# Causal attention of a fused two-layer network: the mask moved from TensorE to VectorE, and score rows cut in their middle

## The chip, the cores and the metric

One core of a Trainium2 chip runs the whole network as one program. The metric is the device time of one execution in microseconds (us). The engines of the core work side by side and meet at semaphores: TensorE (PE in the profile, with its weight loads as PEld), VectorE (DVE), ScalarE (ACT), GpSimd (POOL) and SyncE (SP, which here only issues transfers). TensorE writes to PSUM, eight banks of 512 fp32 columns, from which VectorE and ScalarE read.

## The reference, cut to what matters

The network has two layers with an attention-like half and a mixture-of-experts half each, over 2 batches of 1024 tokens with 256 features. The change lies in the causal attention of the second layer: 16 query heads, 4 key/value heads of 128 features, so four query heads share a key head.

```
scores = jnp.einsum('bqhd,bkhd->bhqk', q, k) / np.sqrt(HD)
causal = jnp.tril(jnp.ones((s, s), dtype=bool))
scores = jnp.where(causal[None, None], scores, jnp.finfo(scores.dtype).min)
probs = jax.nn.softmax(scores, axis=-1)
out = jnp.einsum('bhqk,bkhd->bqhd', probs, v).reshape(b, s, H * HD)
return out @ wo
```

## The kernel before, in words

The program is a sequence of stages (a modulation, a Mamba block, a mixture of experts, attention 1, attention 2, another mixture of experts). Each stage is a block of five engine programs, and the next stage starts when all of them are done. The change is in `attn2`, and in two small casts at the end of `attn1`.

`attn2` works through eight groups u = 0 to 7 (2 batches x 4 key/value heads). In a group each of the four query heads has eight row tiles i = 7 to 0 of 128 queries. Because of the causal mask, row tile i needs only the first (i + 1) x 128 keys, so a score is 128 to 1024 columns wide. One order of work, the list `todo` that `schedule()` writes (tokens project, score, turn, value, out, and a few more), is followed by all engines:

- *score* (line 2362, TensorE): q times k for one head and row tile. Each operand is held as a high and a low part in a rounded fp32 format, and three products (high x high, low x high, high x low) are summed in PSUM. The columns are cut at 512, the size of a bank: 640 columns become 512 + 128, 768 become 512 + 256, 896 become 512 + 384. Then a bf16 matmul of the identity with a 128x128 mask tile (0, and -3e38 above the diagonal) adds the mask to the last 128 columns (line 2365).
- VectorE takes the row maximum of the score from PSUM (line 2145) and scales it by -SCALE (line 2146). ScalarE computes the exponential from PSUM to SBUF with this as bias, and its row sum (line 2247). VectorE takes the reciprocal of the sum (2135, 2137). For three of the heads GpSimd multiplies the row by it (2219), for the fourth VectorE does (2138).
- *turn* (2376): four fp32 transposes of 128x128 probabilities, copied to SBUF by ScalarE (2263). *value* (2386): the product with v, an fp32 matmul that runs as two instructions. *out* (2395): the product with wo, added up by VectorE (2192).
- *project* (2339): the q and k projections of the next group, followed by the rotary embedding on VectorE (2176 to 2178), GpSimd (2203, 2208) and ScalarE (2253).

Scores, projections and their like live in PSUM banks 0 to 3, one or two banks each in turn. A score may start only when the exponential that reads the earlier user of its banks is done (`unit_free`). The transposes of row tile i start when all four heads' probabilities are scaled. VectorE carries further chores between scores, most of them in u = 0: the residual and the normalisation of the other batch.

The mask arrives in fp32 as `mask_f`, loaded during attention 1. Two casts on VectorE at the end of attention 1 (lines 1801 and 1802) make the bf16 mask and the bf16 identity.

Of the kernel before, what the change touches and what calls it, by code (L numbers as in the profile page):

```python
# [7 lines left out]
P = 128  # L8
F32 = mybir.dt.float32
BF16 = mybir.dt.bfloat16  # L10
# [3 lines left out]
ALU = mybir.AluOpType  # L14
ACT = mybir.ActivationFunctionType
AX_X = mybir.AxisListType.X

B, L, D = 2, 1024, 256
# [51 lines left out]
def flat(ap):  # L70
    return ap.rearrange("p a b -> p (a b)")
# [1357 lines left out]
class Ahead:  # L1429
# [3 lines left out]
    def __init__(self, ctx, nc, g, hs):  # L1433
        sb = lambda n, s, d=F32: ctx.enter_context(nc.sbuf_tensor(f"h_{n}", s, d))
        self.hs = hs
        self.hT, self.wh = ([sb(n + half, shape, F32R) for half in ("hi", "lo")] for n, shape in (("hT", [P, KC, L]), ("wh", [P, KC, WC])))
        self.wm, self.qk = ([sb(n + half, [P, c, L], F32R) for half in ("hi", "lo")] for n, c in (("wm", REP - 1), ("qk", KC)))
        self.kT = [q[:, 0, :] for q in self.qk]
        self.qT = [[q[:, 1, :], *(w[:, h, :] for h in range(REP - 1))] for q, w in zip(self.qk, self.wm)]
        self.mask, self.ident_b = sb("mask", [P, P], BF16), sb("ident_b", [P, P], BF16)  # L1440
        sizes = (("w_s", KC * WC), ("cos", L), ("sin", L), ("nwb", D), ("mask_f", P))
        at, part = 0, {}
        for n, size in sizes:
            part[n] = g.raw[:, at:at + size]
            at += size
        self.w_s = part["w_s"].rearrange("p (k n) -> p k n", k=KC)
        self.cos, self.sin, self.nwb, self.mask_f = part["cos"], part["sin"], part["nwb"], part["mask_f"]
        self.spare = g.raw[:, at:at + D]
# [9 lines left out]
def attn1(nc, g, pre, fc_w, fc_b, norm_w, wq, wk, wv):  # L1458
# [7 lines left out]
    with ctx:  # L1466
# [25 lines left out]
        s_nb, s_e, s_eh, s_el, s_vs, s_av, s_acc = sem("nb"), sem("e"), sem("eh"), sem("el"), sem("vs"), sem("av"), sem("acc")  # L1492
        s_rot, s_turned, s_rh, s_roped = sem("rot"), sem("turned"), sem("rh"), sem("roped")
        s_plain = [sem(f"plain{k}") for k in range(KC)]
        s_next, s_nh, s_nl, s_bf = sem("next"), sem("nh"), sem("nl"), sem("bf")
        block = ctx.enter_context(nc.Block())

        def hT_of(b):
# [256 lines left out]
        def _(dve):  # L1755
# [38 lines left out]
            def scaled(q):  # L1794
                if q == 0:
                    own.wait()
                    dve.wait_ge(s_next, 16 * 7)
                norm.scaled(hs[:, TB + 4 * q:TB + 4 * q + 4, :], 4 * q, 4, pre.nwb).then_inc(s_xn, 1)

            def small():  # L1800
                dve.tensor_copy(pre.mask[:, :], pre.mask_f)
                dve.tensor_copy(pre.ident_b[:, :], ident[:, :]).then_inc(s_bf, 1)

            chores = {0: [lambda: stats1(0), lambda: stats1(1), lambda: norm.spread(1, False), lambda: fold(0), lambda: norm.inverse(1, 2),
                          lambda: None, lambda: None, lambda: fold(1),
                          *[lambda q=q: norm.centred(hs, x, TB + 2 * q, 2) for q in range(4)],
# [5 lines left out]
                          *[lambda q=q: norm.modulated(hs, 4 * q, 4, CB, ALU.mult) for q in range(2)],  # L1812
                          *[lambda q=q: norm.modulated(hs, 4 * q, 4, SB, ALU.add) for q in range(2)],
                          lambda: norm.stats(hs, 0, TB), lambda: norm.spread(0, True), lambda: None, lambda: None, lambda: None,
                          lambda: norm.inverse(0, 4), lambda: scaled(0), lambda: (scaled(1), small())]}

            def value_rows(b, h, m):
                r = row[b, h, m]
# [90 lines left out]
def attn2(nc, g, pre, wq, wk, wv, wo):  # L1909
# [8 lines left out]
    with ctx:  # L1918
# [1 line left out]
        sem = lambda n: ctx.enter_context(nc.semaphore(f"a2_{n}"))  # L1920
        x, mod, ps, ident = g.x, g.mod, g.ps, g.ident
        SCALE = 1.0 / float(np.sqrt(HD))
        nrm, hs, nwb, w_s, cos, sin, mask, ident_b = g.nrm, pre.hs, pre.nwb, pre.w_s, pre.cos, pre.sin, pre.mask, pre.ident_b
        wo_s = sb("wo", [P, 2, REP, D])
        HI, LO = 0, 1
        ER = 4
# [4 lines left out]
        e = sb("e", [P, 2, REP, L])  # L1931
        side = sb("side", [P, REP, 5 * P])
        ao = sb("ao", [P, 2, REP, P])
        product = pre.cos.rearrange("p (a d) -> p a d", a=4)
        summed = flat(side[:, :, :])[:, 0:TB * D].rearrange("p (a b) -> p a b", a=TB)
        mx, nb, sm, rc = (sb(n, [P, TB * REP]) for n in ("mx", "nb", "sm", "rc"))
        d_x = nc.dram_tensor("a2_dx", [B * L, D], F32, kind="Internal").ap()
        names = ("own", "acc", "res", "xn", "tr", "hT", "hlow", "whigh", "wlow", "unit", "w", "rot", "sum", "high", "rope", "rope_k",
                 "v", "nb", "e", "rc", "en", "en_last", "xout", "xin", "spare", "wo_in",
                 "tp", "eT", "o", "ao", "wo", "hs")  # L1940
        s = {n: sem(n) for n in names}
        block = ctx.enter_context(nc.Block())
        U = B * KV
# [82 lines left out]
        for t in unit:  # L2026
# [5 lines left out]
            holds.update({c: t for c in banks})  # L2032
            at += size

        def pair(n, w=L, p=slice(0, P)):
            first = home[unit_at[n]]
            return flat(ps[p, first:first + -(-w // 512), :])[:, 0:w]

        def normed(u, i):

# [34 lines left out]
        def _(dve):  # L2075
# [51 lines left out]
                return c  # L2127

            late, extra = [], []

            def normal(u, i, h):
                q = i * REP + h
# [7 lines left out]
            for what, u, i, h in todo:  # L2140
                if what == "score":
                    n = unit[what, u, i, h]
                    q = i * REP + h
                    dve.wait_ge(s["unit"], done[what, u, i, h])
                    own(dve.reduce_max(mx[:, q:q + 1], pair(n, (i + 1) * P), AX_X))  # L2145
                    dve.tensor_scalar(nb[:, q:q + 1], mx[:, q:q + 1], -SCALE, None, ALU.mult).then_inc(s["nb"], 1)  # L2146
                    if late:
                        normal(*late.pop(0))
                    late.append((u, i, h))
                    since = 0  # L2150
                elif what == "turn":
                    if (i, h) == (TB - 1, 0):
                        extra = chores(u)
                    since += 1
                    if late and since == 2:
                        normal(*late.pop(0))
                    elif late and since == 1 and h == i:
                        normal(*late.pop(0))
                    if extra:
                        extra.pop(0)()  # L2160
                elif what == "value":
                    if late and (i, h) == (0, 0):
                        normal(*late.pop(0))
                elif what == "project":
                    n = unit[what, u, i, h]
                    a, b_ = rotated(u)
                    dve.wait_ge(s["unit"], done[what, u, i, h])
                    if u == 1 and i == 0:
                        dve.wait_ge(s["xout"], 16)
                    if u > 0 and i >= 3:  # L2170
                        dve.wait_ge(s["rope"], heads(u, i - 2))
                    elif u > 0 and i == 2:
                        dve.wait_ge(s["rope_k"], u)
                    elif u > 1 or (u, i) == (1, 1):
                        dve.wait_ge(s["rope"], heads(u - 1, REP - 1 + i))
                    dve.tensor_tensor(a[:, i % 2, :], pair(n), cos[:, :], ALU.mult)
                    dve.tensor_tensor(b_[0:64, i % 2, :], pair(n, L, slice(64, P)), sin[64:P, :], ALU.mult)
                    dve.tensor_tensor(b_[64:P, i % 2, :], pair(n, L, slice(0, 64)), sin[0:64, :],  # L2178
                                      ALU.mult).then_inc(s["rot"], 1)
                    if i == 1:  # L2180
                        dve.wait_ge(s["high"], u * NPROJ + 1 - AHEAD)
                        dve.tensor_tensor(kT[LO], a[:, KEY, :], kT[HI].bitcast(F32), ALU.subtract).then_inc(s["rope_k"], 1)
                elif what == "flip":
                    n = unit[what, u, i, h]
                    dve.wait_ge(s["hT"], i + 1)
                    dve.tensor_tensor(hT[LO][:, i, :], pair(n), hT[HI][:, i, :].bitcast(F32), ALU.subtract).then_inc(s["hlow"], 1)
                elif what == "out":
                    c = (u // KV) * TB + i
                    if (u, i) == (KV, TB - 1):
                        dve.wait_ge(s["spare"], 1)  # L2190
                    dve.wait_ge(s["wo"], outs[u, i] + 1)
                    dve.tensor_tensor(hs[:, c, :], ps[:, bank[what, u, i, h], 0:D], hs[:, c, :], ALU.add).then_inc(s["hs"], 1)  # L2192
                    if u == U - 1:
                        extra.append(lambda c=c: finished(c, 1))
# [4 lines left out]
        def _(pool):  # L2199
# [10 lines left out]
            def low_weights(u, c):  # L2210
                at = (slice(None), slice(None), slice(*PIECES[c]))
                pool.wait_ge(s["whigh"], split_until[u - 1] + c + 1)
                pool.tensor_tensor(wh[LO][at], w_s[at], wh[HI][at].bitcast(F32), ALU.subtract).then_inc(s["wlow"], 1)

            for what, u, i, h in todo:
                if what == "score" and h < REP - 1:
                    q, c = i * REP + h, by_pool[scored[u, i, h]]
# [77 lines left out]
        def _(pe):  # L2295
# [22 lines left out]
            for token in todo:  # L2318
# [32 lines left out]
                elif what == "score":  # L2351
# [3 lines left out]
                        if u > 0 or j >= AHEAD - 1:  # L2355
                            pe.wait_ge(s["rope"], heads(u, j + 1))
                    w = (i + 1) * P
                    for t in range(-(-w // 512)):
                        c0, c1 = t * 512, min(w, t * 512 + 512)
                        last = c1 == w  # L2360
                        for x_, y_ in THREE:
                            mm = pe.matmul(ps[:, o + t, 0:c1 - c0], qT[x_][j][:, i * P:(i + 1) * P], kT[y_][:, c0:c1],  # L2362
                                           start=(x_ == y_), stop=(x_ == LO and not last))
                        if last:
                            mm = pe.matmul(ps[:, o + t, c1 - c0 - P:c1 - c0], ident_b[:, :], mask[:, :],  # L2365
                                           start=False, stop=True)
                    mm.then_inc(s["unit"], 1)
                elif what == "turn":
                    if (u, i, j) == (0, TB - 1, 0):
# [124 lines left out]
```

## Time and profile before

| | us |
|---|---|
| median of 3 runs | 2508.93 (2507.75 to 2512.33) |
| the profiled execution | 2510.26 |
| its span | 2508.5 |

| engine | busy us | share of the span |
|---|---|---|
| TensorE, matmuls | 2332.4 | 93% |
| TensorE, weight loads | 1769.5 | 71% |
| VectorE | 1398.5 | 56% |
| ScalarE | 1106.6 | 44% |
| GpSimd | 1120.0 | 45% |

How to read it: the busy shares are means over stages of different kinds, and attention 2 lies between about 1322 and 2204 us of the span. Matmuls overlap in the pipeline, so the duration of a record is longer than the time that the engine needs per matmul; the time from one start to the next is what counts, and the first start behind a longer matmul can be noted early. "Releaser" is the instruction whose end let a waiting one go.

### The profile page before, as it was taken

What the parts mean: (1) busy time and instruction counts of PE and PEld (TensorE: products, weight loads), DVE (VectorE), ACT (ScalarE), POOL (GpSimd) and SP (SyncE); (2) the same over time, 40 slices, a digit from 0 to 9 for tenths busy, and PEclk for the clock granted to TensorE, in tenths of its full rate; (3) what the DMA queues carried; (4) which work ended last, traced back from release to release, by engine and by line L of the source; (5) the groups of instructions that cost most, each with busy time, mean ns of one, the idle gap of its engine ahead of it and who ended that gap; (6) DMA issues with size and microseconds to landing.
All of it is one profiled execution on the core that took longest, in us unless ns stands there. A gap on an engine that the chain in (4) does not pass through costs nothing. (4 is left out here: it accounts for less than half of the span.)

```text
span 2508.5 us, 34038 instructions
## 1 busy us (share of the span) xinstructions
PE 2332.4 (93%) x12534; PEld 1769.5 (71%) x12534; DVE 1398.5 (56%) x2492; ACT 1106.6 (44%) x1886; POOL 1120.0 (45%) x660
## 2 busy tenths in 40 slices
PE   6989999986999988999998999999999999949998
PEld 3368999974777757998896667777776777725554
DVE  4677888874222225545765865566456555453332
ACT  3476777721111114344444454645556464522221
POOL 0457999901323222443454445454545545203443
PEclk8899999997999999999999999999999999979999
DMA  3593362229312221000001000000000001055222
GB/s 114 213 354 109 103 276 78 101 84 304 73 31 32 33 61 35 1 1 1 1 1 53 24 1 19 24 1 20 1 24 1 20 9 34 1 182 144 46 43 32
DMA packets 109620, 168.30 MB, mean 67 GB/s; under 512 B 31250, under 2 KB 78482, under 8 KB 107412
## 3 DMA queue, kind: packets, MB, share of 16 engines
q1 hardware_dynamic: 94484, 145.35, 16.7%
q0 software_dynamic: 14976, 20.78, 5.2%
q8 instruction: 105, 1.72, 0.3%
q14 instruction: 55, 0.45, 0.1%
HBM read 118.57 MB, written 47.60 MB: 66 GB/s over the span
## 5 line engine op out<-in xcount | busy, mean ns | idle before, releaser
L672 POOL TENSOR_TENSOR mb_dbx<-mb_ud,mb_bb 128x1024 f32<-128x1024 f32 x128 | 302.8, 2370 | 76.2 <-DVE mb_h L522 36.7
L522 DVE TENSOR_TENSOR_SCAN mb_h<-ps,mb_dbx 128x1024 f32<-128x1024 f32 x128 | 292.1, 2288 | 59.4 <-ACT ps L635 48.4
L2386 PE MATMUL ps<-a_eT,a_v 128*128 128x512 f32 x576 | 296.5, 597 | 4.8 <-ACT a_eT L2263 4.8
L2219 POOL TENSOR_TENSOR a_e<-a_e,a_rc 128x1024 f32<-128x1024 f32 (+5 forms) x144 | 189.1, 1318 | 248.5 <-DVE a_rc L2135 248.0
L2145 DVE TENSOR_REDUCE a_mx<-ps 128x1 f32<-128x1024 f32 (+7 forms) x256 | 192.6, 752 | 159.3 <-PE ps L2365 158.2
L2263 ACT ACTIVATE a_eT<-ps 128x512 f32<-128x512 f32 x288 | 171.1, 594 | 243.9 <-PE ps L2376 243.2
L815 PE MATMUL ps<-mb_dg,mb_hts 128*128 128x128 f32 x2048 | 252.3, 277 | 5.5 <-DMA mb_dg<-mb_ddiag 5.1
L815 PEld LDWEIGHTS ps<-mb_dg,mb_hts 128*128 128x128 f32 x2048 | 240.8, 194 | 7.2 <-DMA mb_dg<-mb_ddiag 5.4
L1316 DVE COPY e_work<-ps 128x256 f32<-128x256 f32 x78 | 33.1, 425 | 356.0 <-PE ps L1143 356.0
L1891 POOL TENSOR_TENSOR a_elo<-a_e,a_ehi 128x1024 fp32r<-128x1024 f32 x48 | 117.5, 2448 | 215.6 <-ACT a_ehi L1738 110.0
L2247 ACT ACTIVATE a_e<-ps,a_nb 128x1024 f32<-128x1024 f32 (+5 forms) x192 | 156.1, 813 | 81.2 <-DVE a_nb L2146 74.5
L1174 PE MATMUL ps<-e_wd,e_work 128*128 (+1 forms) x780 | 189.1, 385 | 1.9 <-ACT e_work L1073 1.9
L1067 ACT ACTIVATE e_hid<-ps 128x688 f32<-128x688 f32 (+1 forms) x78 | 52.3, 670 | 299.4 <-PE ps L1155 299.4
L1155 PE MATMUL ps<-e_wg,e_work 128*128 x468 | 177.8, 517 | 4.6 <-DVE e_work L1316 1.3
L644 ACT ACTIVATE mb_hts<-ps 128x512 f32<-128x512 f32 x256 | 139.2, 595 | 93.3 <-PE ps L800 93.3
L1155 PE MATMUL ps<-e_wu,e_work 128*128 x468 | 170.3, 500 | 0.0
L1028 POOL DMA_INDIRECT e_acc<-e_hid,e_ids x39 | 61.8, 1585 | 229.1 <-DVE e_hid L1330 229.1
L2362 PE MATMUL ps<-h_qkhi,h_wmhi 128*128 128x512 f32 (+3 forms) x288 | 151.9, 528 | 12.2 <-ACT a_e L2247 5.3
L1174 PEld LDWEIGHTS ps<-e_wd,e_work 128*128 128x128 f32 (+1 forms) x780 | 139.2, 190 | 29.8 <-issue 15.7
L2376 PE MATMUL ps<-ident,a_e 128*128 128x128 f32 x992 | 151.1, 275 | 8.2 <-DVE hs L2192 5.8
L1014 POOL DMA_INDIRECT e_xin<-e_rows,e_ids x78 | 76.9, 987 | 180.3 <-issue 101.1
L2203 POOL TENSOR_TENSOR x<-x 128x1024 f32<-128x1024 f32 x35 | 90.9, 2598 | 135.7 <-DVE x L2178 135.7
(399 smaller groups left out, 5377.5 us busy)
## 6 DMA issues: line engine op xcount, KB each, us to landing
mb_bb<-mb_db_rows SPq DMA_DIRECT2D x16, 1024.0 KB, 9.8
mb_dg<-mb_ddiag SPq DMA_DIRECT2D x15, 1024.0 KB, 12.2
e_wg<-in_g SPq DMA_DIRECT2D x8, 688.0 KB, 9.9
e_wu<-in_u SPq DMA_DIRECT2D x8, 688.0 KB, 11.1
e_wd<-in_d SPq DMA_DIRECT2D x8, 640.0 KB, 10.2
mb_ddiag<-mb_dbx SPq DMA_DIRECT2D x8, 512.0 KB, 3.5
mb_xz<-mb_dxa SPq DMA_DIRECT2D x8, 512.0 KB, 3.7
e_rows<-raw SPq DMA_DIRECT2D x2, 2048.0 KB, 8.7
```

The costliest lines, as they stand in the source:

```text
L522: dve.tensor_tensor_scan(h[:, at % 2, :], pair(at % 2), dbx[:, at % 2, :], 0.0, ALU.mult, ALU.add).then_inc(s_h, 1)
L672: pool.tensor_tensor(dbx[:, at % 2, :], ud[:, kk % 2, 0, :], bb[:, n, :], ALU.mult).then_inc(s_dbx, 1)
L815: mm = pe.matmul(ps[:, 6 + half, q * P:(q + 1) * P], hts[:, at % 2, c:c + P], dg[:, n, c:c + P], start=(n == 0 and q == 0), stop=(n == NS ...
L1155: mm = pe.matmul(ps[:, b0 + a, 0:FN], xT[:, i % 2, k * P:(k + 1) * P], w[:, ds(e), k, a * FN:(a + 1) * FN].rearrange("p a n -> p (a n)"), ...
L1174: mm = pe.matmul(ps[:, 6, 0:D], hT[0:n, i % 2, c * P:(c + 1) * P], wd[0:n, ds(e), c, :].rearrange("p a n -> p (a n)"), start=(c == 0), sto ...
L2145: own(dve.reduce_max(mx[:, q:q + 1], pair(n, (i + 1) * P), AX_X))
L2219: pool.tensor_tensor(probs(i, h), probs(i, h), rc[:, q:q + 1].to_broadcast([P, (i + 1) * P]), ALU.mult).then_inc(s["en"], 1)
L2247: act.activation(probs(i, h), pair(n, (i + 1) * P), ACT.Exp, bias=nb[:, q:q + 1], scale=SCALE, accum_out=sm[:, q:q + 1]).then_inc(s["e"], 1)
L2263: act.activation(eT[:, k % ER, :], ps[:, bank[what, u, i, h], :], ACT.Copy).then_inc(s["eT"], 1)
L2362: mm = pe.matmul(ps[:, o + t, 0:c1 - c0], qT[x_][j][:, i * P:(i + 1) * P], kT[y_][:, c0:c1], start=(x_ == y_), stop=(x_ == LO and not last))
L2376: tr = pe.transpose(ps[:, bank[token], h * P:(h + 1) * P], probs(i, h, j * P, (j + 1) * P), ident[:, :])
L2386: mm = pe.matmul(ps[:, 6 + rows[u, i] % 2, :], v[:, j, u % 2, :], eT[:, k % ER, :], start=(j == 0), stop=(j == i))
```

## The change

The mask is no longer added by TensorE. VectorE adds it while it takes the row maximum: a fused operation reads the score from PSUM and a mask row from SBUF, writes the sum back to the same place in PSUM, and gives the maximum. The mask tile is now 128 x 1024 in fp32, 896 columns of zeros and then the 128 columns of the diagonal tile; a score of width w uses its last w columns. GpSimd fills it at the start of attention 2, and VectorE waits for that before its first work there. The bf16 mask, the bf16 identity, their casts and their semaphore go. Scores of 640, 768 and 896 columns are laid so that the boundary of the two banks is in their middle (`offset`): two pieces of 320, 384 or 448 columns. ScalarE and VectorE read the shifted range.

```diff
-            def small():
-                dve.tensor_copy(pre.mask[:, :], pre.mask_f)
-                dve.tensor_copy(pre.ident_b[:, :], ident[:, :]).then_inc(s_bf, 1)
...
+        mask = sb("mask", [P, L])
...
+        def offset(w):
+            return 512 - w // 2 if 512 < w < L else 0
+
         def pair(n, w=L, p=slice(0, P)):
             first = home[unit_at[n]]
-            return flat(ps[p, first:first + -(-w // 512), :])[:, 0:w]
+            return flat(ps[p, first:first + -(-w // 512), :])[:, offset(w):offset(w) + w]
...
+            dve.wait_ge(s["mask"], 2)
...
-                    own(dve.reduce_max(mx[:, q:q + 1], pair(n, (i + 1) * P), AX_X))
+                    own(dve.tensor_tensor_reduce(pair(n, (i + 1) * P), pair(n, (i + 1) * P), mask[:, L - (i + 1) * P:L], 1.0, -3e38,
+                                                 ALU.add, ALU.max, mx[:, q:q + 1]))
...
+            pool.memset(mask[:, 0:L - P], 0.0).then_inc(s["mask"], 1)
+            pool.tensor_copy(mask[:, L - P:L], pre.mask_f).then_inc(s["mask"], 1)
...
-                    for t in range(-(-w // 512)):
-                        c0, c1 = t * 512, min(w, t * 512 + 512)
-                        last = c1 == w
+                    cut = min(w, 512 - offset(w))
+                    for t, (c0, c1) in enumerate([(0, cut), (cut, w)][:-(-w // 512)]):
+                        at = offset(w) if t == 0 else 0
                         for x_, y_ in THREE:
-                            mm = pe.matmul(ps[:, o + t, 0:c1 - c0], qT[x_][j][:, i * P:(i + 1) * P], kT[y_][:, c0:c1],
-                                           start=(x_ == y_), stop=(x_ == LO and not last))
-                        if last:
-                            mm = pe.matmul(ps[:, o + t, c1 - c0 - P:c1 - c0], ident_b[:, :], mask[:, :],
-                                           start=False, stop=True)
+                            mm = pe.matmul(ps[:, o + t, at:at + c1 - c0], qT[x_][j][:, i * P:(i + 1) * P], kT[y_][:, c0:c1],
+                                           start=(x_ == y_), stop=(x_ == LO))
```

## Rows read from the trace of the kernel before

**Rows 1.** The page's 40 slices: busy tenths of TensorE.
```profile
PE   6989999986999988999998999999999999949998
```

**Rows 2.** Table by stage: stretch, length, busy us of each engine (x instructions), granted clock.
```profile
1322.50:1460.00 137.50, 115.75 (x559) 82.50 (x559) 104.18 (x199) 65.24 (x127) 61.42 (x38) 0.96 0.11 35
1460.00:2198.00 738.00, 733.10 (x3716) 533.12 (x3717) 415.12 (x918) 402.74 (x820) 351.44 (x243) 1.00 0.04 13
```

**Rows 3.** The longest wait of TensorE's matmuls after 1460: total us, times, longest.
```profile
PE ps L2362 <- ACT a_e L2247: 5.2, 8, 1.8
```

**Rows 4.** Timeline of TensorE, a score of 640 columns: start, duration, line, form.
```profile
1724.63 0.40 PE L2362 MATMUL ps<-h_qkhi,h_wmlo 128*128 128x512 f32 x1
1724.87 0.22 PE L2362 MATMUL ps<-h_qkhi,h_wmhi 128*128 128x128 f32 x1
1724.93 0.27 PE L2362 MATMUL ps<-h_qklo,h_wmhi 128*128 128x128 f32 x1
1725.04 0.28 PE L2362 MATMUL ps<-h_qkhi,h_wmlo 128*128 128x128 f32 x1
1725.15 0.23 PE L2365 MATMUL ps<-h_mask,h_ident_b 128*128 128x128 bf16 x1
1725.22 0.61 PE L2376 MATMUL ps<-ident,a_e 128*128 128x128 f32 x4
```

**Rows 5.** The same, two scores of 256 columns back to back.
```profile
1717.46 0.28 PE L2362 MATMUL ps<-h_qkhi,h_wmlo 128*128 128x256 f32 x1
1717.58 0.23 PE L2365 MATMUL ps<-h_mask,h_ident_b 128*128 128x128 bf16 x1
...
1717.83 0.28 PE L2362 MATMUL ps<-h_qklo,h_wmhi 128*128 128x256 f32 x1
```

**Rows 6.** The same, pieces of 384 columns.
```profile
1685.17 0.34 PE L2362 MATMUL ps<-h_qkhi,h_wmhi 128*128 128x384 f32 x1
1685.34 0.35 PE L2362 MATMUL ps<-h_qklo,h_wmhi 128*128 128x384 f32 x1
```

**Rows 7.** Groups by line and form: count, busy us, mean ns, idle before.
```profile
L2176 DVE TENSOR_TENSOR x<-ps,raw 128x1024 f32<-128x1024 f32 x35 | 42.8, 1224 | 82.0 <-POOL h_qklo L2208 32.7 <-POOL h_wmlo L2208 26.6 <-PE ps L2339 22.2
L2146 DVE TENSOR_SCALAR a_nb<-a_mx 128x1 f32<-128x1 f32 x256 | 39.4, 154 | 8.8
L2145 DVE TENSOR_REDUCE a_mx<-ps 128x1 f32<-128x1024 f32 x32 | 39.0, 1219 | 27.4 <-PE ps L2365 27.2
...
L522 DVE TENSOR_TENSOR_SCAN mb_h<-ps,mb_dbx 128x1024 f32<-128x1024 f32 x128 | 292.1, 2288 | 59.4 <-ACT ps L635 48.4
```

**Rows 8.** Timeline of ScalarE: an exponential and the record of its sum.
```profile
1672.75 1.11 ACT L2247 ACTIVATE a_e<-ps,a_nb 128x1024 f32<-128x1024 f32 x1 [0.54 <-PE ps L2376]
1673.76 0.19 ACT L2247 ACTIVATION_READ_ACCUMULATOR a_e<-ps,a_nb 128x1 f32 x1
```

**Rows 9.** Timelines: row 4's last head on VectorE and ScalarE, then TensorE's next.
```profile
1732.85 0.82 DVE L2145 TENSOR_REDUCE a_mx<-ps 128x1 f32<-128x640 f32 x1 [1.49 <-PE ps L2365]
1733.90 0.79 ACT L2247 ACTIVATE a_e<-ps,a_nb 128x640 f32<-128x640 f32 x1
1734.83 0.44 PE L2362 MATMUL ps<-h_qkhi 128*128 128x384 f32 x1
```

**Rows 10.** Timelines: VectorE's scaling of row 7's fourth head, TensorE's transposes of it.
```profile
1683.16 0.76 DVE L2138 TENSOR_SCALAR a_e<-a_e,a_rc 128x1024 f32<-128x1024 f32 x1
1684.01 0.63 PE L2376 MATMUL ps<-ident,a_e 128*128 128x128 f32 x4
```

**Rows 11.** Timelines at the start of attention 2: the first work of VectorE and GpSimd.
```profile
1325.73 1.22 DVE L2176 TENSOR_TENSOR a_e<-ps,raw 128x1024 f32<-128x1024 f32 x1 [9.06 <-PE ps L2339]
1329.50 2.38 POOL L2203 TENSOR_TENSOR a_e<-a_e 128x1024 f32<-128x1024 f32 x1 [8.03 <-DVE a_e L2178]
```

**Rows 12.** Timeline of TensorE: the last matmul of a projection, and transposes.
```profile
1746.62 0.39 PE L2339 MATMUL ps<-h_hThi,h_whlo 128*128 128x512 f32 x1
1746.85 0.60 PE L2376 MATMUL ps<-ident,a_e 128*128 128x128 f32 x4
```

More of the change, by code:

```diff
@@ L1439, in __init__ @@
         self.qT = [[q[:, 1, :], *(w[:, h, :] for h in range(REP - 1))] for q, w in zip(self.qk, self.wm)]
-        self.mask, self.ident_b = sb("mask", [P, P], BF16), sb("ident_b", [P, P], BF16)
         sizes = (("w_s", KC * WC), ("cos", L), ("sin", L), ("nwb", D), ("mask_f", P))
@@ L1494, in attn1 @@
         s_plain = [sem(f"plain{k}") for k in range(KC)]
-        s_next, s_nh, s_nl, s_bf = sem("next"), sem("nh"), sem("nl"), sem("bf")
+        s_next, s_nh, s_nl = sem("next"), sem("nh"), sem("nl")
         block = ctx.enter_context(nc.Block())
@@ L1814, in _ @@
                           lambda: norm.stats(hs, 0, TB), lambda: norm.spread(0, True), lambda: None, lambda: None, lambda: None,
-                          lambda: norm.inverse(0, 4), lambda: scaled(0), lambda: (scaled(1), small())]}
+                          lambda: norm.inverse(0, 4), lambda: scaled(0), lambda: scaled(1)]}
             def value_rows(b, h, m):
@@ L1922, in attn2 @@
         SCALE = 1.0 / float(np.sqrt(HD))
-        nrm, hs, nwb, w_s, cos, sin, mask, ident_b = g.nrm, pre.hs, pre.nwb, pre.w_s, pre.cos, pre.sin, pre.mask, pre.ident_b
+        nrm, hs, nwb, w_s, cos, sin = g.nrm, pre.hs, pre.nwb, pre.w_s, pre.cos, pre.sin
         wo_s = sb("wo", [P, 2, REP, D])
@@ L1939, in attn2 @@
                  "v", "nb", "e", "rc", "en", "en_last", "xout", "xin", "spare", "wo_in",
-                 "tp", "eT", "o", "ao", "wo", "hs")
+                 "tp", "eT", "o", "ao", "wo", "hs", "mask")
         s = {n: sem(n) for n in names}
```

## The prediction

> **What bounds the kernel now.** I read four views, in this order. First the slices of the page, for where TensorE is full: from the 24th slice (some 1440 us) on nearly all are 9s [rows 1]. Then the table by stage, cut where the second attention's first group (a group is one batch and one of its four kv heads; u = 0 to 7 below) gives way to the second, at 1460 us. Third the waits of TensorE after 1460: the longest entry, for ScalarE's exponentials, is 5.2 us in all [rows 3]. So u = 1 to 7 are TensorE's own stream, and a matmul taken out of it shortens the kernel by its slot; u = 0 is paced largely by VectorE and its chores. Last the timeline, for what a slot is: matmuls overlap, so I count from start to start. What follows attention 2 begins only when all its engines are done, so a gain there reaches the end whole.
>
> **What the mask matmuls cost.** There are 256 (8 groups, 4 heads, 8 rows). The one at 1725.15 is followed by the next instruction at 1725.22: 0.066 us in the unrounded trace, though its record is 0.23 long [rows 4]. 25 of a group's 32 stand like that, before transposes or an output. Seven stand before another score: there 0.37 us pass from the last real matmul before the mask (1717.46) to the second behind it (1717.83), where two plain steps of 256 columns (0.12 from 1717.46 to the mask) are 0.235, so 0.13 for the mask [rows 5]; with 128 columns it is 0.07. A group has 25 x 0.066 + some 0.75 = 2.4 us of them, u = 1 to 7 have 16.8 us. Without the mask the transposes' weight load has the last score matmul to hide under; that is at least 0.11 us long, as long as a transpose's own step.
>
> **What the new cut brings.** The steps are 0.233 us for 512 columns (0.24 and 0.23 in the rounded [rows 4, 12]), 0.06, 0.11 and 0.11 for three of 128 (the first one's weights came in under the wide one; the others take no less than 256 columns do) [rows 4], 0.118 for 256 [rows 5] and 0.177 for 384 [rows 6]. Width 640 goes from 3 x 0.233 + 0.28 = 0.98 to six of 320, which between 0.118 and 0.177 I put at 0.148: 0.89. That is 0.09 us, four times a group, 2.6 us over u = 1 to 7. Width 768 goes from 3 x 0.233 + 3 x 0.118 = 1.05 to 6 x 0.177 = 1.06, and 896 from 1.23 to six of 448 at about 0.205, also 1.23: nothing. Sum for TensorE in u = 1 to 7: 19.4 us.
> In u = 0, with at most 2.1 + 0.4 us of the same, I count half, 1.2 us, since much of it falls in front of a wait.
>
> **What VectorE pays.** The reduction over 1024 columns is 1219 ns, a tensor_tensor from PSUM and SBUF over as many 1224 [rows 7]: both one element per cycle, so reading the mask should cost nothing. No row shows the fused operation or VectorE writing to PSUM. Call d what one score's row maximum comes later. The lower end is 0.005 us, the difference of those two rows; the upper end, for an operation at this rate, is a whole small instruction and a hand-over behind it: one small instruction with two hand-overs makes the 0.23 us from the end of a maximum (1733.67) to its exponential [rows 9], and its own 0.154 [rows 7] leaves 0.04 for each, so 0.19. Between them lies the nearest relative, ScalarE's exponential with its accumulator output: it starts at 1672.75, lasts 1.11, and the record that writes the accumulator ends at 1673.95, so 0.09 us behind it [rows 8]. I take d = 0.09, as the mechanism is the same.
> The Trainium skill ("VectorE: DVE Perf Modes", section Two Vector instructions with no wait between them) says that an operation which also writes out its accumulator is two instructions. The trace bears that out on ScalarE alone; with one instruction d would be near the lower end and the sum 3 us better.
>
> **Where d and the faster TensorE meet a wait.** For each score I set its first matmul against the end of the exponential that frees its banks. A TensorE that is really waiting starts 0.14 us behind it. In u = 1 to 7 that is so:
> - at the third head of row 7, in all seven groups. That exponential waits for the last transpose of row 1, not for VectorE, and no mask lies between: unchanged.
> - at the first head of row 2, in all seven. The maximum of row 4's last head starts at 1732.85, its exponential ends at 1734.69, TensorE starts at 1734.83 [rows 9]. Two masks ahead of it go (some 0.2 us), and d comes on top: 7 x (0.2 + 0.09) = 2.0 us.
> - at four single scores (two of row 1, one of row 5, one of row 4): 4 x (0.1 + 0.09) = 0.8 us.
> The transposes of row 7 need VectorE's scaled probabilities of the fourth head, ready at 1683.92 for a start at 1684.01 in four groups [rows 10]; the other four have 5.9 us to spare. 4 x (0.07 + 0.09) = 0.6 us. The next closest is the third head of row 6, with 0.39 us over the 0.14; 0.16 are used.
> In u = 0 VectorE has 32 longer maxima: 32 x 0.09 = 2.9 us, of which some two thirds on the path, 1.9 us.
>
> **Smaller parts.** GpSimd fills the mask tile (896 zeros and 128 copied) before its loop, and VectorE waits for it ahead of its own. VectorE's first operation there is at 1325.73, and the stage opens at 1322.4 [rows 11]. A GpSimd operation over 1024 columns with two inputs takes 2.4 us [rows 11], so even at that price the tile is there at about 1324.9 or, with a copy of 0.4 behind it, 1325.2; cost 0. If it came later, each microsecond would go onto u = 0. GpSimd's first sum waits for VectorE until 1329.5 anyway. The two casts gone from attention 1 are some 0.4 us of VectorE where it waits for scores: 0. SP's queue is not touched.
>
> **Sum.** 19.4 + 1.2 - 2.0 - 0.8 - 0.6 - 1.9 = 15.3 us. The profiled execution took 2510.26 us, its span 2508.5; it becomes about 2495. The median of the three timed runs is 1.3 us below it, 2508.9, so the forecast is 2494.
>
> **Rivals.**
> A. *The waits swallow nothing* (d near 0, exponentials of row 2 in time, all masks of u = 0 on the path): 16.8 + 2.6 + 2.5 = 22 us, 2487. For it, VectorE has 44% of its time free after 1460 [rows 2]; against it, the seven waits of [rows 9]. Chance 0.10.
> B. *The fused operation has a long fixed part*, as an operation of this kind may. Losses grow as 36 d (7 + 4 + 4 waits and 21 of u = 0) beside the 2.1 us that the removed masks expose: at d = 0.3 they are 12.9 of 20.6, 2501; at d = 0.5 nothing is left. Against it: every small operation of VectorE here is 0.15 to 0.17. Chance 0.17, a third of it with no gain to be seen.
> C. *The fused operation runs at half rate and the kernel gets slower.* VectorE's scan, also a running result fed back from PSUM data, takes 2288 ns for 1024 columns [rows 7], 1.07 more than the reduction, so 1.04 ns more per column. Then u = 0 loses 32 x 0.69 x 0.65 = 14.4 us, row 2's wait 7 x 0.96 = 6.7, row 7's transposes 4 x 1.23 = 4.9, row 6's third head 7 x 0.7 = 5.0 (its 0.39 us are gone) and the four others 2.8: 33.8 against 20.6, 2522. It decides from d = 0.5 on. For it, only the scan; against it, the reduction has feedback too and runs at full rate. Chance 0.09.
> D. *The mask slots are not freed*, because weight loads fill them: TensorE's weight loads are busy 533 of 738 us [rows 2]. Then only width 640 pays, and the waits of d stay: about 2508. Against it: a projection's last 512-column matmul and the transpose behind it stand 0.23 us apart, the matmul's own step, with the same kinds of weights loaded [rows 12]. Chance 0.04.
>
> **Numbers.** The forecast has 0.60, with its own range 2490 to 2499. The range 2487 to 2505 leaves out C, D and the worse part of B. A measurement of this kernel tells 0.2% (5 us) from no change. Faster by more: the forecast, A and two thirds of B, 0.82. Within 0.2%: D and most of the rest of B, 0.08. Slower: C and a little of B, 0.10.
>
> **What the profile after would show.** No bf16 matmul of 128 columns in the score line, and the step from the last score matmul to the transposes 0.12 to 0.23 us. Width 640 as six matmuls 0.145 to 0.15 apart. The new VectorE record over 1024 columns near 1.22 us, followed by one of about 0.15, and the scaling by -SCALE 0.09 later than now. The stretch from 1460 shorter by some 15 to 16 us, u = 0 within 1.5 us of now. TensorE's waits for exponentials up from 5.2 to about 8. I would be wrong if the fused record is over 1.5 us for 1024 columns, or if TensorE's busy share after 1460 falls below 97%.

## The result and the profile after

The changed kernel takes 2496.0 us (median of 5 runs, 2493.5 to 2498.6) and the one before, timed on the same chip in turn with it, 2509.9 (5 runs, 2507.8 to 2512.6): a ratio of 0.9943, 95% interval 0.9929 to 0.9958. The forecast was 2494, its range 2487 to 2505.

The page of the changed kernel. The slices are those of [rows 1]; the other lines are the page's total and the new line of the fused operation.

```profile
span 2494.2 us, 33783 instructions
...
PE 2314.1 (93%) x12278; PEld 1773.4 (71%) x12278; DVE 1411.8 (57%) x2746; ACT 1105.7 (44%) x1886; POOL 1123.1 (45%) x662
...
PE   6988999986999988999998989999999999949998
...
L2146 DVE CUSTOM_DVE_ANT_0 ps<-ps,a_mask 128x1024 f32<-128x1024 f32 (+7 forms) x256 | 194.5, 760 | 134.7 <-PE ps L2366 133.1
```

The table by stage of the changed kernel, in the columns of [rows 2]. The second stretch ends at 2181, where attention 2 is as far along as it was at 2198.

```profile
1322.80:1460.00 137.20, 114.32 (x524) 83.56 (x524) 106.02 (x232) 64.70 (x125) 62.48 (x40) 0.94 0.11 35
1460.00:2181.00 721.00, 712.92 (x3491) 535.16 (x3491) 424.81 (x1140) 402.23 (x822) 353.36 (x243) 1.00 0.04 13
2181.00:2494.20 313.20, 264.19 (x974) 155.43 (x974) 118.89 (x329) 62.05 (x137) 100.20 (x78) 0.92 0.38 90
```

The middle stretch is 17 us shorter and holds 225 fewer matmul records (seven groups have 224 mask matmuls, and a record can be missing). TensorE is busy for 98.9% of it. VectorE has 222 more instructions there (the accumulator reads) but under 10 us more of work.

The waits of TensorE in that stretch, as in [rows 3]:

```profile
PE ps L2366 <- ACT a_e L2251: 6.9, 17, 1.8
PE ps L2387 <- ACT a_eT L2267: 1.6, 3, 1.0
PE ps L2396 <- ACT a_ao L2289: 0.7, 1, 0.7
```

A score of 640 columns in the changed kernel, to be set against [rows 4]. TensorE's timeline: six matmuls of 320 columns, no mask behind them.

```profile
1718.84 0.31 PE L2366 MATMUL ps<-h_qklo,h_wmhi 128*128 128x320 f32 x1
1718.98 0.31 PE L2366 MATMUL ps<-h_qkhi,h_wmlo 128*128 128x320 f32 x1
1719.13 0.30 PE L2366 MATMUL ps<-h_qkhi,h_wmhi 128*128 128x320 f32 x1
1719.27 0.31 PE L2366 MATMUL ps<-h_qklo,h_wmhi 128*128 128x320 f32 x1
1719.42 0.31 PE L2366 MATMUL ps<-h_qkhi,h_wmlo 128*128 128x320 f32 x1
1719.57 0.27 PE L2377 MATMUL ps<-ident,a_e 128*128 128x128 f32 x1
```

They start 0.146 us apart (median in the unrounded trace), and the transposes follow one such step later. The other steps, measured the same way, are 0.112 for 128 columns, 0.119 for 256, 0.175 for 384, 0.203 for 448 and 0.233 for 512.

What VectorE pays, first by form, then as it happens (a row 7 score in u = 0). Both views are of the changed kernel.

```profile
L2146 DVE CUSTOM_DVE_ANT_0 ps<-ps,a_mask 128x1024 f32<-128x1024 f32 x32 | 39.3, 1227 | 24.8 <-PE ps L2366 24.8
L2146 DVE DVE_READ_ACCUMULATOR2_ANT a_mx<- 128x1 f32 x256 | 35.9, 140 | 0.0
L2146 DVE CUSTOM_DVE_ANT_0 ps<-ps,a_mask 128x640 f32<-128x640 f32 x32 | 26.6, 831 | 24.8 <-PE ps L2366 24.4
```

```profile
1332.80 1.23 DVE L2146 CUSTOM_DVE_ANT_0 ps<-ps,a_mask 128x1024 f32<-128x1024 f32 x1 [1.59 <-PE ps L2366]
1333.95 0.14 DVE L2146 DVE_READ_ACCUMULATOR2_ANT a_mx<- 128x1 f32 x1
1334.12 0.15 DVE L2148 TENSOR_SCALAR a_nb<-a_mx 128x1 f32<-128x1 f32 x1
1334.19 0.15 DVE L2136 RECIPROCAL a_rc<-a_sm 128x1 f32<-128x1 f32 x1
```

The fused operation takes 1227 ns where the reduction took 1219 [rows 7]. The accumulator read has a record of 140 ns, but starts before the main one's record ends. The scaling starts 1.32 us after the operation; it started 1.26 us after the reduction. So d, by which each maximum comes later, is 0.065 us. This also bears out what the Trainium skill says in "VectorE: DVE Perf Modes", section Two Vector instructions with no wait between them: an operation that writes out its accumulator is two instructions. On VectorE it is, and the second costs 0.065 us, half of its record of 0.140.

**Where the span's 14.3 us come from.** I cut each trace at three events instead of at round times: the first projection of attention 2, the first transposes of row 7 in u = 1, and the last output. Below, u = 0 is the part from the first to the second, "the stretch" from the second to the third. Each value is worked out from the start and end times of those matmuls.

```
kernel             u=0      stretch   behind attention 2
before             147.24   732.82    305.71
changed            147.38   716.06    307.79
```

The stretch gains 16.8 us, u = 0 loses 0.1, what lies behind loses 2.1, and the start before attention 2 another 0.3.

Nothing was edited behind attention 2. The difference there goes with the clock. The 25 us behind the last output, first in the kernel before, then in the changed one, then in the kernel of experiment 1 (the granted clock is the third value from the end):

```profile
2203.10:2228.10 25.00, 14.32 (x64) 7.37 (x64) 15.49 (x43) 8.89 (x15) 0.00 (x0) 0.80 0.72 228
```

```profile
2186.40:2211.40 25.00, 13.91 (x56) 6.83 (x56) 15.57 (x42) 7.59 (x13) 0.00 (x0) 0.73 0.72 229
```

```profile
2189.00:2214.00 25.00, 15.49 (x65) 7.67 (x63) 15.57 (x42) 8.02 (x14) 0.00 (x0) 0.80 0.74 229
```

TensorE waits some 9 to 11 us for VectorE there in all of them and comes back at the lower level, 1.2 GHz. In the changed kernel the clock is at that level for 3.5 us longer (0.73 against 0.80 of 25 us), and 56 matmuls fit in instead of 64. Experiment 1 has the same code there, a clock of 0.80 and 305.5 us behind attention 2. Over the kernels below this part lies between 304.7 and 308.1 us with the same code in it. So most of the 2 us is time at the lower clock, in code that the change doesn't touch. But it may be more than scatter: the second trace of the changed kernel (experiment 8) has the same 0.73 there and 308.1 us, and none of the other kernels has it. Whether the changed kernel brings it about, and why the clock comes back earlier in the others, is open.

### The profile page after: what moved, and what is told of

It reads as the page before. It is cut to its first block and busy times, and to the rows that moved or that the text cites. A ratio compares the mean times of both kernels' runs of the same rounds, so it can differ in the third digit from the quotient of the medians.

```text
span 2494.2 us, 33783 instructions
## 1 busy us (share of the span) xinstructions
PE 2314.1 (93%) x12278; PEld 1773.4 (71%) x12278; DVE 1411.8 (57%) x2746; ACT 1105.7 (44%) x1886; POOL 1123.1 (45%) x662
## 5 line engine op out<-in xcount | busy, mean ns | idle before, releaser
L2146 DVE CUSTOM_DVE_ANT_0 ps<-ps,a_mask 128x1024 f32<-128x1024 f32 (+7 forms) x256 | 194.5, 760 | 134.7 <-PE ps L2366 133.1
L2366 PE MATMUL ps<-h_qkhi,h_wmhi 128*128 128x384 f32 (+5 forms) x288 | 149.1, 518 | 13.2 <-ACT a_e L2251 5.9
L2377 PEld LDWEIGHTS ps<-ident,a_e 128*128 128x128 f32 x992 | 122.9, 142 | 48.4 <-issue 32.4
## 6 DMA issues: line engine op xcount, KB each, us to landing
mb_dg<-mb_ddiag SPq DMA_DIRECT2D x15, 1024.0 KB, 12.4
```

The source lines that it names most:

```text
L2146: own(dve.tensor_tensor_reduce(pair(n, (i + 1) * P), pair(n, (i + 1) * P), mask[:, L - (i + 1) * P:L], 1.0, -3e38, ALU.add, ALU.max, mx[:, ...
L2366: mm = pe.matmul(ps[:, o + t, at:at + c1 - c0], qT[x_][j][:, i * P:(i + 1) * P], kT[y_][:, c0:c1], start=(x_ == y_), stop=(x_ == LO))
L2377: tr = pe.transpose(ps[:, bank[token], h * P:(h + 1) * P], probs(i, h, j * P, (j + 1) * P), ident[:, :])
```

## The experiments

Each kernel's ratio is to the kernel before on the same chip, with its 95% interval. The kernel before took 2513.1 us beside experiments 1 to 4, 2513.7 beside 5, 7, 8 and 9, and 2514.8 beside 6 and 10, so whole times here are 3 to 5 us above those of the result, and above the expected ones largely for that. Differences in parts come from one trace each. The granted clock is 1.00 over the whole stretch in all of them. Cuts in the code are marked by three dots.

**1. The mask moved, the cut left as it was.** Scores of 640 columns are again 512 + 128.

```diff
-            return 512 - w // 2 if 512 < w < L else 0
+            return 0
```

> The changed kernel with its score rows cut at column 512 again, as before; the mask is still added by VectorE. I read the stretch of groups u = 1 to 7, from the first transposes of row 7 in u = 1 to the end of TensorE's last output matmul: 732.8 us before, 716.1 after. Theory: the removed mask slots pay 16.8 us less some 2.7 of waits there, the cut 2.6, independent of each other. Then the stretch is 718.7 us and the whole about 2498.5. Rival: the mask slots were filled by weight loads anyway and the cut brought nearly all; then the stretch is about 730 and the whole near 2508.

Measured: 2499.4 us, ratio 0.9947 (0.9932 to 0.9961), stretch 719.5, u = 0 146.1. Against the kernel before, the stretch is 13.3 us shorter. The prediction's terms give 16.8 - 2.0 - 0.8 - 0.6 = 13.4.

**2. The new cut alone.** Mask matmuls and plain reduction as before, the boundary in the middle.

```diff
-                    for t in range(-(-w // 512)):
-                        c0, c1 = t * 512, min(w, t * 512 + 512)
+                    cut = min(w, 512 - offset(w))
+                    for t, (c0, c1) in enumerate([(0, cut), (cut, w)][:-(-w // 512)]):
+                        at = offset(w) if t == 0 else 0
...
+                            mm = pe.matmul(ps[:, o + t, at + c1 - c0 - P:at + c1 - c0], ident_b[:, :], mask[:, :],
```

> The kernel before with the cut in the middle alone; the mask stays a bf16 matmul on TensorE. Theory: width 640 gains 0.09 us four times a group, widths 768 and 896 nothing: stretch 730.2 us instead of 732.8, the step between pieces of 320 columns 0.148 us, whole about 2507. Rival (the cut brought nearly all): stretch about 719.

Measured: 2510.3 us, ratio 0.9992 (0.9983 to 1.0002), stretch 729.8: 3.05 us, where 2.6 were predicted. By the time alone it can't be told from nothing; only the trace shows it (the shift of the read range, `offset`, is as in the change and not shown). The two parts add up to 16.4 of the 16.8 us.

**3. The mask left out altogether** (this kernel computes attention 2 without its causal mask): mask matmuls gone, plain reduction, old cut.

```diff
-                        if last:
-                            mm = pe.matmul(ps[:, o + t, c1 - c0 - P:c1 - c0], ident_b[:, :], mask[:, :],
-                                           start=False, stop=True)
```

> The kernel before without its mask matmuls; the mask is left out of the computation, the row maximum is the plain reduction. It is the first experiment without the fused operation, so the two differ only by d, the 0.065 us that the row maximum comes later there. Theory: d costs 15 waits x 0.065 = 1.0 us in the stretch and up to 1.4 us in u = 0: stretch 717.7 if the first experiment gives 718.7, u = 0 about 146 us instead of 147.4, whole about 2496. Rival A: the fused operation costs nothing at all, then both stretches are equal. Rival B: writing the sum back to PSUM slows TensorE or ScalarE, then this one is 3 us or more ahead.

Measured: 2500.1 us, ratio 0.9952 (0.9939 to 0.9965), stretch 717.6. In the stretch experiment 1 differs from it only by the fused operation, so d costs 1.9 us there. The prediction had 15 waits x 0.09 = 1.35. I laid the two traces over each other at the first transpose of every step: row 2's first head loses 0.08 us in each of the seven groups, 0.6 in all, and the rest falls at places that differ by group, most of it in u = 3, 5 and 7. Elsewhere TensorE's steps are the same to some 0.01 us, so no slowing by VectorE's writes to PSUM is to be seen. The whole kernels can't be told apart, as the clock's scatter is larger.

**4. The slot put back on TensorE.** Experiment 1 plus, behind each score, a bf16 matmul of 128 columns that adds zeros (TensorE also waits once for the mask tile, ahead of its first score).

```diff
+                        last = c1 == w
...
+                        if last:
+                            mm = pe.matmul(ps[:, o + t, c1 - c0 - P:c1 - c0], mask[:, 0:P // 2].bitcast(BF16), mask[:, 0:P // 2].bitcast(BF16),
+                                           start=False, stop=True)
```

> The first experiment with the slot on TensorE given back: a bf16 matmul of zeros by zeros onto the last 128 columns of each score, while VectorE adds the mask and takes the maximum in the fused operation. Against the kernel before it differs only by d. Theory: stretch 732.8 + 1.0 = 733.8 us or a little less (TensorE has less to lose where it is not waiting), u = 0 up to 1.4 us longer than 147.2, whole 2510 to 2513. Rival B (VectorE's PSUM writes disturb others): 736 or more. Rival (the zero matmul hides): near 719.

Measured: 2517.4 us, ratio 1.0013 (1.0004 to 1.0022), stretch 734.4. The slots are worth 14.9 us (the prediction's 16.8 less the 2.1 that the waits take, 14.7). With them back the kernel is no faster than the one before, and its stretch is 1.5 us longer: the fused operation by itself is a small loss. The whole gain of the mask's move is what TensorE no longer does. Rival D, slots that aren't freed, is out. So is C, half rate, by the 1227 ns above.

**5. The maximum later still.** One more small VectorE instruction between maximum and scaling, 0.19 us each.

```diff
-                    dve.tensor_scalar(nb[:, q:q + 1], mx[:, q:q + 1], -SCALE, None, ALU.mult).then_inc(s["nb"], 1)
+                    own(dve.tensor_scalar(mc[:, q:q + 1], mx[:, q:q + 1], 1.0, None, ALU.mult))
+                    dve.tensor_scalar(nb[:, q:q + 1], mc[:, q:q + 1], -SCALE, None, ALU.mult).then_inc(s["nb"], 1)
```

> The changed kernel with one more small VectorE operation per score, a copy of the row maximum between the fused operation and the scaling by -SCALE: d grows from 0.065 by about 0.19 us. Theory: a later maximum costs only where TensorE already waits, 15 places in u = 1 to 7, so the stretch grows from 716.1 by 15 x 0.19 = 2.9 us to 719.0, and by up to 1.5 more where row 6's third head (0.11 to 0.34 us to spare now) runs out; u = 0 grows by 21 x 0.19 = 4.0 us. Whole about 2503. Rival: attention 2 is now bound by the chain over VectorE throughout, then each of the 224 later maxima costs its 0.19, 42 us; or VectorE has room everywhere, then nothing.

Measured: 2508.9 us, ratio 0.9983 (0.9974 to 0.9991), stretch 724.1, u = 0 151.6. This was a miss. u = 0 lost 4.3 us, as expected, but the stretch lost 8.1, far more than expected. An instruction of VectorE does two things: it delays its own score's exponential, and it delays whatever stands behind it in VectorE's queue. In u = 1 to 7 the prediction counted the first only. The next experiment parts them.

**6. The same instruction behind the scaling.** Its own score's maximum is as early as in the changed kernel; only the queue is longer.

```diff
+                    own(dve.tensor_scalar(mc[:, q:q + 1], mx[:, q:q + 1], 1.0, None, ALU.mult))
```

> The same extra small VectorE instruction for each score as in e5, but behind the scaling by -SCALE instead of ahead of it: the row maximum of its own score isn't later, only what VectorE does next. Stretches as in e1: u = 0 from the first projection to the first transposes of row 7 of u = 1, then from there to the last output (the changed kernel: 147.4 and 716.1; e5: 151.6 and 724.1). Theory 1 (what counts is how late a maximum reaches its exponential, by its own chain): nothing is left of e5's loss but where two scores follow each other at once, stretch 716 to 718, u = 0 below 149. Theory 2 (VectorE is behind in places, several scores in a row, and each extra operation lengthens its queue there): at least half of e5's 8.0 us stays, stretch 720 to 724, u = 0 about 149 to 151.

Measured: 2502.8 us, ratio 0.9958 (0.9942 to 0.9974), stretch 720.1, u = 0 150.7. So 4.1 of the 8.1 us come from the queue alone; the other 4.0 I put down to the score's own chain, which takes the two to add up. In u = 0 3.3 of the 4.3 are queue. They don't add up everywhere: at a value matmul some 15 us into u = 3 the queue alone costs as much as both. TensorE's timeline of the changed kernel, of experiment 5 and of this one:

```profile
1694.13 1.13 PE L2387 MATMUL ps<-a_eT,a_v 128*128 128x512 f32 x2 [0.32 <-ACT a_eT L2267]
```

```profile
1702.99 1.13 PE L2389 MATMUL ps<-a_eT,a_v 128*128 128x512 f32 x2 [0.74 <-ACT a_eT L2269]
```

```profile
1700.16 1.12 PE L2389 MATMUL ps<-a_eT,a_v 128*128 128x512 f32 x2 [0.74 <-ACT a_eT L2269]
```

The value waits for ScalarE's copy of the transposed probabilities, and that copy stands behind an exponential which waits for VectorE. VectorE comes to that score straight from a chore. Experiment 5, VectorE and then ScalarE:

```profile
1698.31 2.29 DVE L1412 SCALAR_TENSOR_TENSOR x<-hs,n_rstd,raw 128x256 f32<-128x256 f32 x2
1700.51 0.69 DVE L2147 CUSTOM_DVE_ANT_0 ps<-ps,a_mask 128x512 f32<-128x512 f32 x1
```

```profile
1701.67 0.69 ACT L2253 ACTIVATE a_side<-ps,a_nb 128x512 f32<-128x512 f32 x1 [1.73 <-DVE a_nb L2150]
1702.35 0.59 ACT L2269 ACTIVATE a_eT<-ps 128x512 f32<-128x512 f32 x1
```

The place that costs most is another, and the prediction doesn't have it: the value matmul just ahead of row 4's first score, before row 5's first transposes. It starts 0.46 us behind the transposes ahead of it in the changed kernel, 0.75 in experiment 5 and 0.57 in this one. Laid over the changed kernel, experiment 5 loses 0.3 to 0.4 us from there to row 5's first transposes in each of the seven groups, 2.7 in all, and this one 0.2 to 0.4, 1.8 in all. VectorE has four scores in a row there (three of row 1, one of row 0). In the changed kernel it idles 0.32 us ahead of the fourth; in experiment 5 no idle time is left between them (it would stand in brackets), so each extra 0.19 us is handed on. Experiment 5, u = 2:

```profile
1616.59 0.41 DVE L2147 CUSTOM_DVE_ANT_0 ps<-ps,a_mask 128x256 f32<-128x256 f32 x1
...
1617.28 0.15 DVE L2150 TENSOR_SCALAR a_nb<-a_mc 128x1 f32<-128x1 f32 x1
1617.35 0.15 DVE L2137 RECIPROCAL a_rc<-a_sm 128x1 f32<-128x1 f32 x1
1617.42 0.41 DVE L2147 CUSTOM_DVE_ANT_0 ps<-ps,a_mask 128x256 f32<-128x256 f32 x1
```

At the first head of row 2 it is the other way round. From the last matmul of the score ahead to the second of row 2's there are 0.73 us in the changed kernel and in this one, and 0.92 in experiment 5, where two plain steps make 0.29: the 0.19 are the score's own chain, in all seven groups.

**7. A wait filled.** The third head of row 7 waits for its banks in all seven groups. It was scored ahead of row 0's transposes of the group before; it is now scored behind them.

```diff
+                if u + 1 < U and i == 0:
+                    put("score", u + 1, 7, 2)
...
-                            if i < 2:
-                                put("score", u + 1, 7, 2 * (1 - i) + j)
+                            if i == 1:
+                                put("score", u + 1, 7, j)
```

> The changed kernel with the third head's row-7 score of the next group issued behind the transposes of row 0 instead of in front of them. In every group from u = 1 on TensorE stands 0.57 us in front of that score, until the exponential of the first head frees its banks; 0.44 us of transposes now fill it. Theory: 7 x 0.44 = 3.1 us less, stretch 713.0 (the last group has no next, u = 0 has one), whole about 2493. Rival: the score comes 0.44 us later on VectorE, and the fourth head behind it makes the transposes of row 7 wait longer in u = 1, 3, 5, 7; then less than 1.5 us are left.

Measured: 2495.4 us, ratio 0.9937 (0.9925 to 0.9950), stretch 714.5 against 716.1 of the changed kernel. The wait is gone, but only u = 1, 3 and 5 get shorter by it (0.43, 0.66 and 0.41 us). In u = 2, 4 and 6, which end at the row 7 transposes of u = 3, 5 and 7, those transposes now come 0.57 us late for want of VectorE's scaling, where it had been 0.20 (against their plain step of 0.21 in the other groups). These are the groups that the prediction named for that wait [rows 10]. So the rival is right on the mechanism, and 1.6 us are left where it had less than 1.5.

**8. The changed kernel again.** No edit.

> The changed kernel itself, for its time on the same chip beside the others. Both theories expect 0.994 of the kernel before; the stretch of u = 1 to 7 at 716.1 us within 0.5, as TensorE runs at full clock there, while u = 0 and what lies outside attention 2 vary by 1 to 2 us with where the clock falls.

Measured: 2496.8 us, ratio 0.9941 (0.9928 to 0.9953), stretch 716.1, behind it 308.1. The stretch repeats to 0.04 us, so differences of 0.5 us in it can be read.

**9. Row 2 one step later.** On top of experiment 7, all four scores of row 2 stand just ahead of the transposes of row 5's last step. Two of them stood there already; the first two move there, one step later.

```diff
-                     ... [(p, 2, h) for h, p in enumerate((4, 4, 5, 5))]}
+                     ... [(p, 2, h) for h, p in enumerate((5, 5, 5, 5))]}
```

> As the sixth experiment, and all four scores of row 2 one transpose step later, just ahead of the last transposes of row 5, so that the exponential of row 4's last head has 1.3 us more until its banks are wanted. Theory: the wait of 0.36 us in front of row 2 goes, 2.5 us, and part of it comes back where the next projection waits for the exponentials of row 2: stretch 711 to 713. Rival: VectorE has four maxima in a row there, about 3.6 us of work against 2 us of TensorE's, and the projection waits 1 us or more: stretch 717 or more.

Measured: 2493.6 us, ratio 0.9926 (0.9913 to 0.9939), stretch 713.0. This is the lowest time of all; its interval overlaps that of the changed kernel, its stretch is 3.1 us shorter, 1.5 of them by this step. Laid over experiment 7, the seven groups gain 3.0 us up to row 5's last transposes, and some 1.6 come back by the first two transposes of row 4, half of that in u = 7 alone. The 713.0 are the upper edge of what was expected. The place of row 2's first head, on TensorE's timeline of the changed kernel and then of this one:

```profile
1728.51 0.28 PE L2366 MATMUL ps<-h_qkhi,h_wmlo 128*128 128x128 f32 x1
1728.96 0.45 PE L2366 MATMUL ps<-h_qkhi 128*128 128x384 f32 x1 [0.17 <-ACT a_e L2251]
```

```profile
1729.77 1.02 PE L2389 MATMUL ps<-a_eT,a_v 128*128 128x512 f32 x2
1730.22 0.74 PE L2368 MATMUL ps<-h_qkhi 128*128 128x384 f32 x1
```

**10. One score more ahead of row 7's transposes.** In experiment 9 these transposes come some 0.55 us late in u = 1, 3, 5 and 7. The second head of row 6 is put in front of them.

```diff
-            ahead = {7: [(p, 6, h) for h, p in enumerate((0, 1, 2, 3))] + ...
+            ahead = {7: [(p, 6, h) for h, p in enumerate((0, 0, 2, 3))] + ...
```

> e8, and the second head of row 6 is scored ahead of row 7's first transposes instead of behind them (1.05 us of TensorE there). In e8 those transposes wait 0.53 us for VectorE in u = 1, 3, 5 and 7. If the wait is only filled: stretch 712.95 - 2.1 = 710.8. Rival: the banks of that score come free too late (they belong to row 7's heads, whose exponentials are just running), the wait moves ahead to the score and the stretch stays at 713 or gets longer, up to 4 x 1 us.

Measured: 2499.0 us, ratio 0.9941 (0.9924 to 0.9958), stretch 718.8, 5.8 us longer than in experiment 9, u = 0 as there (147.3). Neither expectation met it. The transposes no longer wait, nor does the moved score. The wait came up one matmul further, at the value matmuls. The waits of TensorE, first in experiment 9 (1460 to 2178 us), then in this one (1460 to 2183):

```profile
PE ps L2368 <- ACT a_e L2253: 2.5, 4, 1.4
PE ps L2389 <- ACT a_eT L2269: 2.0, 3, 1.0
```

```profile
PE ps L2389 <- ACT a_eT L2269: 8.9, 10, 1.1
PE ps L2368 <- ACT a_e L2253: 2.5, 4, 1.4
```

The timelines of TensorE and of ScalarE in this kernel (u = 3) show how:

```profile
1681.97 1.03 PE L2379 MATMUL ps<-ident,a_e 128*128 128x128 f32 x8
1684.15 1.13 PE L2389 MATMUL ps<-a_eT,a_v 128*128 128x512 f32 x2 [1.14 <-ACT a_eT L2269]
```

```profile
1682.51 1.01 ACT L2253 ACTIVATE a_e<-ps,a_nb 128x896 f32<-128x896 f32 x1 [2.15 <-DVE a_nb L2150]
1683.42 0.19 ACT L2253 ACTIVATION_READ_ACCUMULATOR a_e<-ps,a_nb 128x1 f32 x1
1683.51 0.59 ACT L2269 ACTIVATE a_eT<-ps 128x512 f32<-128x512 f32 x1
```

Without a score between the first two steps, TensorE makes eight transposes at once and then needs their copy. The copy stands in ScalarE's queue behind row 6's exponential, 1.01 us, which had itself waited for VectorE. The score between them had been the cover for that.

## Why the prediction was right

Its mechanism held: TensorE's stream in u = 1 to 7 gets shorter by the slots of the masks and by the cut of width 640, and the later maximum takes a little back at waits. That the terms of the later maximum came out near is in part luck, as two of their factors were off in opposite ways.

- *Masks, 16.8 us less what the waits swallow.* Right: 13.4 predicted in the stretch, 13.3 measured (experiment 1); the slots themselves 14.7 and 14.9 (experiment 4).
- *The cut, 2.6 us.* 3.05 alone (experiment 2). With the steps measured above, width 640 gives 0.979 - 0.876 = 0.103 us (0.09 was predicted), and the widths 768 and 896, put at nothing, give 0.006 each: 28 x 0.115 = 3.2 us.
- *d = 0.09.* It is 0.065: two records, as forecast, the second 0.140 us (about 0.15 was forecast).
- *What d costs.* The step with the wrong size, though it hid behind a d that was too high. The prediction had 15 waits in the stretch and 21 us per us of d in u = 0 ("losses grow as 36 d"). Measured are (8.1 + 4.3)/0.19 = 65 us per us (experiment 5), and 39 of them are queue (experiment 6: (4.1 + 3.3)/0.19). What the prediction lacked is VectorE's queue in u = 1 to 7, above all the value ahead of row 5's transposes. In the stretch it is 43 instead of 15; in u = 0 it is 23, so there the guess of 21 was right, and mostly as queue, as it was meant. So d was a third too high and the losses nearly twice as steep. At the d of the change the two errors roughly cancel (1.9 us in the stretch by experiment 3, 1.35 predicted; it is less than 43 x 0.065 = 2.8; row 5's place, with 0.4 us a group in experiment 5, loses 0.12 in u = 3 and nothing in the other groups at this d, as spare time covers it). For rival B they don't cancel. With experiment 5 at d = 0.25 and a ratio of 0.9983, and 12.4 us lost of the 16.6 that stretch and u = 0 had gained, the gain is gone at about d = 0.3 and not at 0.5, by an estimate along that line; no run has such a d.
- *The waits of row 2 and row 7's transposes.* Both are there. TensorE's wait for exponentials is 6.9 us, up from 5.2; about 8 was forecast. The transposes come 0.20 us late in four groups, where 0.16 was forecast.
- *u = 0.* A loss of 0.7 was forecast (1.2 gained, 1.9 lost), 0.1 is measured. The clock differs here and has to be told apart: over u = 0 it is granted at 0.97 in the kernel before, at 0.94 in the changed one and in experiments 2 and 3, and at 0.98 in 1 and 4. At the same 0.98, experiment 4 has 147.0 and experiment 1 146.1, so the masks are worth 1.0 us there. At the same 0.94, the changed kernel has 147.4 and experiment 3 146.6, so d less the new cut costs 0.8. The forecast had 1.0 (half of 2.1) and 1.7 (1.9 less half of 0.4). The 0.1 us lost against the kernel before is at unequal clocks.
- *The mask fill.* Free, as predicted. GpSimd, changed kernel:

```profile
1322.94 0.85 POOL L2217 MEMSET a_mask<- 128x896 f32 x1 [1.18 <-POOLq L1465]
1323.74 0.28 POOL L2218 COPY a_mask<-raw 128x128 f32<-128x128 f32 x1
```

It is done at 1324.0, and VectorE's first operation there starts at 1326.1, held by a projection as before.

The stretch gained 16.8 us where the prediction's terms make 16.0, so net of u = 0 attention 2 gained 16.6 instead of 15.3. For the profiled execution 2495 was forecast, and it took 2496.0 (span 2494.2): the 1.3 us more from attention 2 were outweighed by 2.1 us behind it and 0.3 ahead of it, which the prediction had left unchanged. That the two nearly cancel is luck too. It is also the median of the five runs, while the forecast of 2494 took the median to lie 1.3 us below it.

## What to carry to other kernels

Where a matmul engine's stream sets the pace, count start-to-start steps and take matmuls out of it, even if that makes another engine's work longer: here 256 slots of some 0.066 us against 256 x 0.065 us on VectorE gave 13 us (experiment 1). But an added instruction on a half-idle engine is not free. Multiply it by the waits at which its own result is late *and* by the places where the engine runs several items in a row; put the same instruction behind the result to tell the two apart. And look at what a piece of work covers before moving it: of the three waits filled here two came back in part, and one more than whole, at the next consumer.

## What the hardware showed that I had not expected

- A fused add and maximum that reads PSUM and SBUF and writes PSUM runs at the reduction's rate: 1227 ns for 1024 columns, 831 for 640, 292 for 128, so about 1.04 ns per column.
- A 140 ns accumulator read adds only 0.065 us to the chain, since it starts 0.08 us before the main record ends.
- Matmuls of 128 columns step at 0.112 us and those of 256 at 0.119, while from 256 to 512 the step doubles (0.233). So the narrow piece of 512 + 128 costs nearly as much as one of 256. That is why 320 + 320 pays, while for 768 and 896 the cut is worth 0.006 us a score.
